# Layers of a transformer on one core: each engine's order rewritten tile by tile

## The reference, cut to what matters

```python
for i in range(6):
    x = attn_layer(shift_tokens(x), Wqkv[i], q_scale[i], k_scale[i], Wo[i]) + x
    x = ffn_layer(shift_tokens(x), ln_g[i], ln_b[i], W1[i], b1[i], W2[i], b2[i]) + x
```

## Time and profile before

| | |
|---|---|
| runs, median (lowest to highest) | 3695.51 us (3693.23 to 3698.8), 3 runs |
| profiled execution, span from the first to the last instruction | 3699.1 us |
| mean granted clock of TensorE | 0.987 |
| busy share: TensorE, its weight loads, VectorE, ScalarE, GpSimd | 95%, 73%, 82%, 70%, 62% |
| instructions on the same | 63940, 63940, 4947, 4028, 1364 |
| layers' first product, last deviation step | 599.3 us, 3661.9 us |

### The profile page before, as it was taken

How to read it: one execution, slowest core, us unless ns; L and a number is a source line. 1 busy time by engine, 2 the same in 40 slices (tenths; PEclk the granted TensorE clock), 3 DMA queues, 4 the chain that set the end, 5 groups by cost and what they waited for, 6 DMA issues and landing times. The chain is left out here.

```text
span 3699.1 us, 146879 instructions
## 1 busy us (share of the span) xinstructions
PE 3521.4 (95%) x63940; PEld 2694.0 (73%) x63940; DVE 3039.5 (82%) x4947; ACT 2586.6 (70%) x4028; POOL 2309.1 (62%) x1364
## 2 busy tenths in 40 slices
PE   6999996999999999999999999999999999999996
PEld 4777774777777777777777777777777777777774
DVE  5767766988889988888888888888898888888883
ACT  3565554677777777777777777777777777777773
POOL 1110104767777777777777767777777777776761
PEclk9999998999999999999999999999999999999998
DMA  2000001212222222222222222222222222222212
GB/s 75 4 4 7 4 7 43 56 48 58 56 58 63 64 56 58 56 56 62 58 56 58 54 56 64 56 58 55 64 63 58 56 57 54 56 56 54 54 49 68
DMA packets 121989, 188.76 MB, mean 51 GB/s; under 512 B 24942, under 2 KB 43142, under 8 KB 120972
## 3 DMA queue, kind: packets, MB, share of 16 engines
q1 hardware_dynamic: 121356, 179.36, 18.7%
HBM read 24.08 MB, written 4.19 MB: 8 GB/s over the span
## 5 line engine op out<-in xcount | busy, mean ns | idle before, releaser
L1325 POOL TENSOR_TENSOR rc<-rc,rs 128x1024 f32<-128x1024 f32 x384 | 912.9, 2377 | 349.2 <-DVE rs L1391 348.5
L1331 POOL TENSOR_TENSOR rc<-rc,rnorm 128x1024 f32<-128x1024 f32 x384 | 723.7, 1906 | 392.9 <-DVE rnorm L162 331.4
L1385 DVE TENSOR_TENSOR rc<-proj,rope_b 128x1024 f32<-128x1024 f32 x384 | 466.7, 1215 | 96.1 <-ACT squares L1177 89.6
L1177 ACT ACTIVATE squares<-proj 128x1024 f32<-128x1024 f32 x384 | 394.0, 1026 | 151.1 <-PE proj L921 137.6
L1013 PEld LDWEIGHTS ring<-pT,vmoved 64*64 64x64 f32 x18432 | 381.2, 135 | 132.8 <-issue 132.8
L1391 DVE TENSOR_TENSOR rs<-proj,rope_b 128x1024 f32<-128x1024 f32 x384 | 466.2, 1214 | 0.0
L958 PEld LDWEIGHTS ring<-ident,rc 128*128 128x128 f32 x3072 | 364.2, 142 | 137.5 <-issue 52.2
L1399 DVE TENSOR_REDUCE sums<-squares 128x16 f32<-128x1024 f32 x384 | 455.3, 1186 | 1.1 <-issue 0.9
L1013 PE MATMUL ring<-pT,vmoved 64*64 64x32 f32 x18432 | 407.7, 220 | 37.9 <-issue 36.4
L958 PE MATMUL ring<-ident,rc 128*128 128x128 f32 x3072 | 426.3, 277 | 11.6 <-POOL rc L1331 6.6
L1013 PE MATMUL ring<-pT,vown 64*64 64x32 f32 x6144 | 381.9, 219 | 13.8 <-issue 13.8
(11 more groups left out here) (176 smaller groups left out, 7886.1 us busy)
## 6 DMA issues: line engine op xcount, KB each, us to landing
vmoved<-vown SPq DMA_DIRECT2D x576, 128.0 KB
vmoved<-vown SPq DMA_DIRECT2D x192, 192.0 KB
vmoved<-vown SPq DMA_DIRECT2D x576, 64.0 KB
wqkv_raw<-in_L_ffn_Wqkv SPq DMA_DIRECT2D x40, 192.0 KB, 2.7
wo<-in_L_ffn_Wo SPq DMA_DIRECT2D x6, 512.0 KB, 4.2
x_attended<-xtok SPq DMA_DIRECT2D x8, 256.0 KB, 2.0
xtok_c<-x_attended SPq DMA_DIRECT2D x8, 256.0 KB, 4.2
out<-xtok_c SPq DMA_DIRECT2D x8, 256.0 KB, 2.4
```

The lines of the kernel that those rows point to most:

```text
L1177: nc.scalar.activation(squares[:, c, :], proj[c][:, :], ACT.Square).then_inc(sq_done, 1)
L1325: nc.gpsimd.tensor_tensor(rc[:, k % 2, c, :], rc[:, k % 2, c, :], rs[:, c, :], ALU.add).then_inc(add_done, 1)
L1331: nc.gpsimd.tensor_tensor(dst, dst, rnorm[:, k % 2, c * HEADS:(c + 1) * HEADS].rearrange("p (h o) -> p h o", o=1).broadcast_to([P, HEADS, ...
L1385: nc.vector.tensor_tensor(rc[:, k % 2, c, :].rearrange("p (h d) -> p h d", h=HEADS), proj[c][:, :].rearrange("p (h d) -> p h d", h=HEADS), ...
```

## The change

The loops over steps `g` are replaced by loops over rounds `n` (one per sequence), in which each engine's list is written out for the four tiles one by one, with its own place for every step. Where a step of one tile used to have the same neighbours as that of the next, all differ now. The semaphores `proj_full`, `sq_done`, `ss_done`, `turned_done`, `add_done` and `unit_done` become two each, one for q and one for k, since these no longer alternate. Every step waits for its own needs (`values` for the staged input, `score` for both of its transposes, `turned` and `after` for the borrowed halves of `proj`). `weigh` is issued whole. The ninth weight chunk is split ahead of the loops on ScalarE and GpSimd. In the lists of ScalarE and GpSimd a round is written one sequence later than in TensorE's. The operations, their shapes and the DMAs are the same. The core of the diff:

```diff
-LAST_STEP = NT + 6
+ROUNDS = range(-1, NSEQ + 2)
 
 
 def ring_order():
 
     out = []
-    for g in range(-1, LAST_STEP + 1):
-        mine = [("T3", g - 1), ("V0", g - 1), ("P0", g - 2), ("P1", g - 2), ("V1", g - 1), ("O0", g - 2), ("O1", g - 2),
-                ("T0", g), ("T1", g), ("T2", g)]
+    for n in ROUNDS:
+        mine = [("O0", 4 * n), ("O1", 4 * n), ("T0", 4 * n + 2), ("T1", 4 * n + 2), ("P0", 4 * n + 1),
+            ("V0", 4 * n + 2), ("T3", 4 * n + 2), ("P1", 4 * n + 1), ("O0", 4 * n + 1), ("O1", 4 * n + 1),
+            ("T3", 4 * n + 3), ("V1", 4 * n + 2), ("T0", 4 * n + 3), ("T2", 4 * n + 3), ("T1", 4 * n + 3),
+            ("V0", 4 * n + 3), ("V1", 4 * n + 3), ("P0", 4 * n + 2), ("P1", 4 * n + 2), ("T2", 4 * n + 4),
+            ("T3", 4 * n + 4), ("O0", 4 * n + 2), ("O1", 4 * n + 2), ("T1", 4 * n + 4), ("T0", 4 * n + 4),
+            ("P0", 4 * n + 3), ("P1", 4 * n + 3), ("O0", 4 * n + 3), ("O1", 4 * n + 3), ("V0", 4 * n + 4),
+            ("V1", 4 * n + 4), ("T0", 4 * n + 5), ("T2", 4 * n + 5), ("T3", 4 * n + 5), ("V0", 4 * n + 5),
+            ("T1", 4 * n + 5), ("P0", 4 * n + 4), ("V1", 4 * n + 5), ("P1", 4 * n + 4), ("T2", 4 * n + 6)]
         out += [(name, k) for name, k in mine if 0 <= k < NT]
     return out
 
@@ -801,9 +807,9 @@
         w_hi_done = sem("w_hi_done"); w_lo_done = sem("w_lo_done")
...
-        proj_full = sem("proj_full"); sq_done = sem("sq_done"); ss_done = sem("ss_done")
-        straight_done = sem("straight_done"); turned_done = sem("turned_done"); add_done = sem("add_done")
-        clamp_done = sem("clamp_done"); rn_done = sem("rn_done"); unit_done = sem("unit_done")
+        proj_full = [sem(f"proj_full{c}") for c in range(2)]; sq_done = [sem(f"sq_done{c}") for c in range(2)]; ss_done = [sem(f"ss_done{c}") for c in range(2)]
+        straight_done = sem("straight_done"); turned_done = [sem(f"turned_done{c}") for c in range(2)]; add_done = [sem(f"add_done{c}") for c in range(2)]
+        clamp_done = sem("clamp_done"); rn_done = sem("rn_done"); unit_done = [sem(f"unit_done{c}") for c in range(2)]
...
+            def turned(c, k):
+
+                if k >= 0:
+                    pe.wait_ge(turned_done[c], min(k, NT - 1) + 1)
+
+            def after(sem, per, n, i):
+
+                if n >= 0:
+                    pe.wait_ge(sem, per * min(n, NSEQ - 1) + i)
...
+            for n in ROUNDS:
+                weigh(4 * n)
+                after(ffn_read, 1, n - 2, 1)
+                turned(0, 4 * n + 3)
+                mean(n - 1)
+                transpose_qk(4 * n + 2, 0)
+                project(1, 4 * n + 4)
+                transpose_qk(4 * n + 2, 1)
+                after(centred, 1, n - 1, 1)
+                after(ffn_read, 1, n - 2, 1)
+                turned(0, 4 * n + 3)
+                variance(n - 1)
+                transpose_probs(4 * n + 1, 0)
+                score(4 * n + 2, 0)
+                values(4 * n + 2, 0)
+                transpose_qk(4 * n + 2, 3)
+                after(var_read, 1, n - 1, 1)
+                after(centred, 1, n - 1, 1)
+                after(ffn_read, 1, n - 2, 1)
+                project(0, 4 * n + 4)
+                transpose_probs(4 * n + 1, 1)
+                score(4 * n + 2, 1)
+                weigh(4 * n + 1)
+                project(1, 4 * n + 5)
+                transpose_qk(4 * n + 3, 3)
+                values(4 * n + 2, 1)
+                turned(0, 4 * n + 4)
+                spread(n - 1)
+                transpose_qk(4 * n + 3, 0)
+                turned(0, 4 * n + 4)
+                output(n, 0)
+                transpose_qk(4 * n + 3, 2)
+                transpose_qk(4 * n + 3, 1)
+                after(normed, 1, n - 1, 1)
+                after(attn_added, 2, n, 1)
+                project(0, 4 * n + 5)
+                values(4 * n + 3, 0)
+                values(4 * n + 3, 1)
+                score(4 * n + 3, 0)
+                score(4 * n + 3, 1)
+                transpose_probs(4 * n + 2, 0)
+                transpose_probs(4 * n + 2, 1)
+                turned(0, 4 * n + 5)
+                feed_up(n - 1, 3)
+                transpose_qk(4 * n + 4, 2)
+                transpose_qk(4 * n + 4, 3)
+                turned(0, 4 * n + 5)
+                feed_up(n - 1, 0)
+                weigh(4 * n + 2)
+                turned(1, 4 * n + 5)
+                feed_up(n - 1, 1)
+                turned(1, 4 * n + 5)
+                feed_up(n - 1, 4)
+                transpose_qk(4 * n + 4, 1)
+                transpose_qk(4 * n + 4, 0)
+                after(gated, 3, n - 1, 1)
+                after(gelu_done, 3, n - 1, 1)
+                project(0, 4 * n + 6)
+                transpose_probs(4 * n + 3, 0)
+                after(gated, 3, n - 1, 2)
+                turned(1, 4 * n + 5)
+                feed_up(n - 1, 2)
+                transpose_probs(4 * n + 3, 1)
+                score(4 * n + 4, 0)
+                score(4 * n + 4, 1)
+                weigh(4 * n + 3)
+                after(gelu_done, 3, n - 1, 3)
+                after(gated, 3, n - 1, 2)
+                after(gelu_done, 3, n - 1, 2)
+                project(1, 4 * n + 6)
+                values(4 * n + 4, 0)
+                values(4 * n + 4, 1)
+                turned(0, 4 * n + 6)
+                feed_up(n - 1, 5)
+                transpose_qk(4 * n + 5, 0)
+                transpose_qk(4 * n + 5, 2)
+                turned(0, 4 * n + 6)
+                output(n, 1)
+                transpose_qk(4 * n + 5, 3)
+                values(4 * n + 5, 0)
+                after(attn_added, 2, n, 2)
+                after(gated, 3, n - 1, 3)
+                project(0, 4 * n + 7)
+                transpose_qk(4 * n + 5, 1)
+                project(1, 4 * n + 7)
+                transpose_probs(4 * n + 4, 0)
+                values(4 * n + 5, 1)
+                score(4 * n + 5, 0)
+                score(4 * n + 5, 1)
+                transpose_probs(4 * n + 4, 1)
+                transpose_qk(4 * n + 6, 2)
+                turned(0, 4 * n + 7)
+                feed_down(n - 1)
...
+                    return
                 if n >= BATCH:
                     act.wait_ge(res_done, n - BATCH + 1)
+                if n:
+                    k = TILES * (n - 1) + 2 * half + 1
+                    act.wait_ge(proj_full[1], k + 1)
+                    act.wait_ge(ring_full, RING["V1", k] + 1)
...
 
             def values_out(k, b):
+                if not tile(k):
+                    return
+                if k > 1:
+                    act.wait_ge(ring_full, RING["O1", k - 2] + 1)
                 if b == 0:
...
+            act.wait_ge(raw_in, 16)
+            act.wait_ge(w_lo_done, BATCH)
+            split_hi(BATCH, w_raw[:, :])
+
+            for n in ROUNDS:
+                exponentials(4 * n - 3)
+                attention_out(4 * n - 4, 0)
+                mask_scores(4 * n - 2)
+                attention_out(4 * n - 4, 1)
+                squared_deviation(n - 2)
+                qk_out(4 * n - 2, 0)
+                qk_out(4 * n - 2, 1)
+                squares_of(1, 4 * n)
+                probs_out(4 * n - 3, 0)
+                values_out(4 * n - 2, 0)
+                qk_out(4 * n - 2, 3)
+                widen_deviation(n - 2)
+                probs_out(4 * n - 3, 1)
+                squares_of(0, 4 * n)
+                attention_out(4 * n - 3, 0)
+                attention_out(4 * n - 3, 1)
+                qk_out(4 * n - 1, 3)
+                values_out(4 * n - 2, 1)
+                mask_scores(4 * n - 1)
+                exponentials(4 * n - 2)
+                qk_out(4 * n - 1, 0)
+                scale_shift(n - 2)
+                squares_of(1, 4 * n + 1)
+                qk_out(4 * n - 1, 2)
+                qk_out(4 * n - 1, 1)
+                squares_of(0, 4 * n + 1)
+                values_out(4 * n - 1, 0)
+                values_out(4 * n - 1, 1)
+                stage_hi(n, 1)
+                probs_out(4 * n - 2, 0)
+                probs_out(4 * n - 2, 1)
+                qk_out(4 * n, 2)
+                qk_out(4 * n, 3)
+                exponentials(4 * n - 1)
+                gelu(n - 2, 0)
+                attention_out(4 * n - 2, 0)
+                attention_out(4 * n - 2, 1)
+                gelu(n - 2, 1)
+                qk_out(4 * n, 1)
+                mask_scores(4 * n)
+                qk_out(4 * n, 0)
+                probs_out(4 * n - 1, 0)
+                squares_of(0, 4 * n + 2)
+                probs_out(4 * n - 1, 1)
+                gelu(n - 2, 2)
+                attention_out(4 * n - 1, 0)
+                attention_out(4 * n - 1, 1)
+                squares_of(1, 4 * n + 2)
+                values_out(4 * n, 0)
+                values_out(4 * n, 1)
+                exponentials(4 * n)
+                next_hi(n)
+                qk_out(4 * n + 1, 0)
+                qk_out(4 * n + 1, 2)
+                mask_scores(4 * n + 1)
+                qk_out(4 * n + 1, 3)
```

(111 more changed lines are left out.)

482 lines of the change are left out of this document (202 added, 280 removed).

## The result

The change makes the kernel slower by 8.5%: 4013.9 us against 3697.2 us in runs side by side, ratio 1.085 (95% interval 1.084 to 1.087). The forecast was slower by 1.5%, 3751 us, with a range up to 3830. The sign was right; the size, and most of the cause, were not.

What follows compares the result with a forecast made beforehand. TensorE's list was taken as the bound, 60.9 us undisturbed. 60.9 - 1.15 - 0.3 + 0.2 + 4.0 + 0.4 = 64.05 us per sequence, +49 over 47 periods, +55 with the start: 3751 us, range 3640 to 3830.

Steps and rivals of the forecast that it cites:

- Period and stall terms: TensorE's sequence: 63.0 us, being 60.9 undisturbed plus 2.1, of which 1.70 are instruction-loading stalls in `weigh` and `score`.
- Steps 1 and 2: TensorE per sequence: five fewer runs of small products save 1.15 us; the wait of `project(0)` behind the gate saves 0.3.
- Step 3: New waits between engines: lists of 59.4 us (TensorE) and 56.1 (VectorE) fit a period just under 60; charged 0.2 us.
- Step 4: Longer dense runs of `weigh` and `score` on TensorE raise instruction-loading stalls from 1.70 to 4.0 us per sequence, +2.3.
- the sum: All per-sequence terms together: 64.05 us, +1.05 per sequence, with 0.4 for everything else as before.
- Step 5: Kernel start: ScalarE and GpSimd wait for the ninth weight chunk before the first staging, about +6 us once.
- Loading hidden: TensorE's instruction loading costs no more than before: 61.75 us per sequence, 3643 us in all; chance 0.25.
- The added wait for the seven copies: ScalarE's `values_out(4n+5,0)` waits for tile 4n+4's copies; 0.5 to 1.4 us per sequence reach TensorE, about 3800 us; chance 0.10.
- The sign by which the prediction called itself wrong: TensorE idling on semaphores of ScalarE or GpSimd for more than 1 us per sequence would refute the forecast.
- The other such sign, stalls below 2.8: TensorE's instruction-loading stalls staying below 2.8 us per sequence would refute the forecast.
- The idle time in `score`: TensorE's idle time without a releaser in `score`, 13.6 us in 30 pieces before, would at least double.

Runs made afterwards that it cites:

- the last experiment: Kernel after with one-input small norm operations (norms left out), 2560 TensorE instructions per sequence and 86 unused increments ahead of the loops: 3635.5 us, ratio 0.984.
- one-input operations: Kernel after with each of the nine small operations of `norms_of` replaced by a `tensor_reduce` reading one SBUF tile, norms left out: 3809.8 us, ratio 1.032.
- the last two experiments: Kernel after with one-input small norm operations and 2560 TensorE instructions per sequence, with 109 or 86 increments ahead of the loops: 3762.1 and 3635.5 us.
- the aligned kernel: Kernel before without TensorE's redundant `sq_done` wait (2560 instructions per sequence) and with 73 unused increments ahead of its loops: 3611.2 us, ratio 0.977.

## Why the prediction was wrong, point by point

- **Period and stall terms (what bounds the kernel).** Right. 60.9 undisturbed plus 2.1 of instruction loading: with the block ends placed, the old order runs at 61.08, without a stop.
- **Steps 1 and 2, fewer changes of shape, a wait gone (-1.45).** Right within about 0.3 as a sum; no run tests the two terms one by one. In the last experiment the period of 61.30 less its stops (51.8 us with the 0.21 each, 1.13 per sequence) and the 0.29 leaves 59.9, 1.2 under the old order's 61.08. And with one-input operations one sequence, 61.01 us long, has TensorE busy 59.43 at a clock of 1.00, where the lists laid end to end gave 59.4 (the first line below; the second is the slowest sequence):

```profile
859.65:920.66 61.01, 59.43 (x1254) 47.18 (x1253) 53.30 (x85) 46.38 (x72) 47.29 (x28) 1.00 0.23 58
1898.56:1971.33 72.77, 66.84 (x1258) 52.15 (x1257) 53.27 (x84) 47.53 (x73) 46.07 (x26) 0.91 0.19 49
```

- **Step 3, new waits: the step that failed.** It laid VectorE's list end to end with durations of before, "2.3 for the norms", to 56.1, and concluded that "the order fits a period just under 60"; further down it expected "VectorE, ScalarE and GpSimd with the same busy time per sequence". The duration of the norms was a property of the old order, in which GpSimd mostly stood still beside them. In the new one they take 9.7 us more per sequence. VectorE's list is then 56.4 + 9.3 = 65.7 with its own gaps, past TensorE's, and becomes the bound; 204 us went there. The 3.7 from there to the period of 69.42 are waits of VectorE for others, a third of them for `output` (62.4 us). The edge that the step charged most for, `project(0,4n+5)` behind `add_attention`, was put at 0.3 with the old durations and took 1.5; it too is gone with one-input operations. A sign stood in the trace of before: the clamp had a mean of 383 ns beside 192 for its like, and `rtmp<-rtmp,sums` of 36 columns 514.
- **Step 4, density: +2.3, right in size with VectorE's lateness taken away.** In the kernel after the stops were 2.85 instead of 4.0. I take it that TensorE's other waits gave the next block time to arrive; no run shows that by itself. With one-input operations they were

```profile
PE ring L1043 <- issue: 126.3, 109, 2.2
PE scr L1007 <- issue: 30.1, 37, 1.5
```

that is (156.4 + 146 x 0.21) / 46 = 4.07. The rule behind the number (instructions of a run beyond 180) was not tested, and since a placement alone moves the stops from 2.7 us a sequence to 1.1, as the last two experiments show, there is luck in so near a hit.
- **What the sum left out.** With the blocking gone the period is 65.23, not 64.05. Behind some of the stops the granted clock falls. First the timeline of TensorE at one of them in the one-input kernel, then windows of 4 us around it:

```profile
1914.53 0.33 PE L1043 MATMUL ring<-pT,vmoved 64*64 64x32 f32 x3 [1.50 <-issue]
...
1915.10 2.93 PE L1093 MATMUL proj<-xc,w 128*128 128x512 f32 x3
```

```profile
1910.00:1914.00 4.00, 3.03 (x119) 2.13 (x117) 3.96 (x5) 3.95 (x5) 0.00 (x0) 1.00 0.02 4
1914.00:1918.00 4.00, 3.48 (x18) 1.86 (x19) 2.02 (x3) 1.88 (x4) 3.65 (x2) 0.57 0.41 89
1918.00:1922.00 4.00, 4.00 (x24) 2.83 (x23) 2.33 (x10) 2.75 (x5) 3.62 (x3) 1.00 0.40 112
```

A clock of 0.57 over a slice is mostly the 1.2 GHz level, 1.00 the 2.4 GHz level; the fall comes with the end of the stop, not ahead of it. The three `feed_up` products behind this stop took 2.93 us; at 1522.41 in the kernel after, at a clock of 1.00, two take 1.02. The slowest sequence, 72.77 us at 0.91, has TensorE busy 66.84, 7.4 more than the 59.43 above for the same products. By the trace's clock, TensorE stood at the lower level for 130 us of these 46 sequences, for 20 in the kernel before and not at all in the aligned kernel. On the mean 65.23 - 59.43 - 4.07 leaves 1.7 for this and the rest, where I had put 0.4; half of 130 us, 1.4 per sequence, is my estimate of the clock's share.
- **Step 5, the start: +6.** It was 9.8 with one-input operations (the first multiplication at 736.95), 15.3 in the kernel after.
- **The rivals and signs.** Loading hidden: no, stalls rose by 1.15 in the kernel after, just over the 1.1 that was to decide, and by 2.4 with one-input operations. The added wait for the seven copies is there, on ScalarE (45.8 us in 53 pieces, 1.0 per sequence, 43.4 with one-input operations) but hardly reaches TensorE: its waits for `vown` come to 3.3 us in all (2.4 with one-input operations). The sign by which the prediction called itself wrong did appear: 67.2 us of TensorE's waits are for ScalarE's `pT`, 1.5 per sequence. They were a relay of VectorE's lateness, and are gone with one-input operations. The other such sign, stalls below 2.8, was escaped by 0.05. The idle time in `score` did not double as expected (21.7 us after 13.6; 30.1 with one-input operations). None of the rivals had an engine whose instructions grow.

## What to carry to other kernels

When an order is rewritten, a duration read from the old trace may belong to the old neighbours. Ask of each short VectorE operation with two SBUF inputs what GpSimd does at that moment in the new order: nine small ones took 2 us or 6 here by that alone. Compare busy time per engine first: here the same work had more busy time, and the table of waits did not name the cause. And where TensorE issues many small products, count its instructions per loop round: a multiple of 256 with the block ends in a good place was worth 2.3% here with no change of the work, where a whole new order lost 8.5%.

## What the hardware showed that I had not expected

- A VectorE operation of 0.19 us with two SBUF operands takes up to 2.29 us beside a 2.35 us GpSimd add, and 0.19 beside a 2.24 us memset. The GpSimd adds themselves did not lengthen (mean 2377 ns in the earlier trace rows; the pair above takes 4.70 together).
- TensorE's stops for instructions stand at block ends, every 256th instruction, and most of the last 256 are then `score` or `weigh` (on the median 253 in the kernel after, 225 in the one before); the aligned kernel crosses block ends with up to 226 of them without a stop. The longest is 2.4 us in the kernel after, and in the slow sequences some microseconds at the lower clock follow. With a fixed placement all but one of the aligned kernel's 46 periods are 60.66 to 61.31 or 62.2 us, where those of before went from 60.9 to 66.
